# Mixture of experts over tokens sorted by expert: items of two weight chunks and 256 tokens, in place of every expert over every token

## What is computed

```python
h = x @ down_w + down_b                          # 512 -> 256
logits = x @ router_w + router_b - COST_LAMBDA * cost
probs = jax.nn.softmax(logits, axis=-1)
topv, topi = jax.lax.top_k(probs, TOP_K)         # TOP_K = 2
gate = jax.nn.softmax(topv, axis=-1)
for k in range(TOP_K):
    mask = jax.nn.one_hot(topi[..., k], E, dtype=h.dtype)
    acc = jnp.zeros_like(h)
    for e, (w1, b1, w2, b2) in enumerate(expert_params):
        hm = h * mask[..., e:e + 1]
        acc = acc + (_gelu(_gelu(hm) @ w1 + b1) @ w2 + b2)
    out = out + acc * gate[..., k:k + 1]
out = out + 0.1 * (_gelu(_gelu(h) @ shared_w1 + shared_b1) @ shared_w2 + shared_b2)
out = out @ up_w + up_b
out = out + (_gelu(x) @ core_w + core_b)
```

## Time and profile before

| | us |
|---|---|
| median of 3 runs (3240.45 to 3253.45) | 3247.59 |
| the profiled execution | 3248.38 |
| its span, first to last instruction | 3246.5 |
| the block of the mixture in it | 622.1 to 1317.6 |
| its loop over pairs | 791.4 to 1267.0 |
| PE busy over the whole span | 2938.1 (91%) |

### The profile page before, as it was taken

How to read it: one execution, slowest core, us unless ns; L and a number is a source line. 1 busy time by engine, 2 the same in 40 slices (tenths; PEclk the granted TensorE clock), 3 DMA queues, 4 the chain that set the end, 5 groups by cost and what they waited for, 6 DMA issues and landing times. The chain is left out here.

```text
span 3246.5 us, 44385 instructions
## 1 busy us (share of the span) xinstructions
PE 2938.1 (91%) x13909; PEld 1804.4 (56%) x13932; DVE 2050.6 (63%) x4083; ACT 1539.4 (47%) x3166; POOL 279.6 (9%) x248
## 2 busy tenths in 40 slices
PE   8999978799999999699899899898799999993887
PEld 4455444335999997465566655654555454432333
DVE  5666554343566665675765756755577777856776
ACT  5445332222555554254344344443477676754454
POOL 0000012002000000110210200201110101000010
PEclk9999999898999999899999999999999999995999
DMA  3000004100000000300000000000100000004000
GB/s 123 14 13 0 13 30 134 46 29 5 12 13 10 13 11 2 149 1 1 14 1 14 1 1 14 1 1 5 48 8 5 5 5 2 2 2 156 7 19 26
DMA packets 42490, 77.63 MB, mean 24 GB/s; under 512 B 6256, under 2 KB 21376, under 8 KB 39392
## 3 DMA queue, kind: packets, MB, share of 16 engines
q1 hardware_dynamic: 39440, 67.40, 5.9%
q0 software_dynamic: 2896, 8.31, 0.8%
HBM read 55.25 MB, written 4.19 MB: 18 GB/s over the span
## 5 line engine op out<-in xcount | busy, mean ns | idle before, releaser
L1890 DVE TENSOR_REDUCE x_neg_max<-bank 128x1 f32<-128x512 f32 x512 | 327.4, 684 | 95.4 <-PE bank L1735 94.8
L1842 ACT ACTIVATE x_weights<-bank 128x512 f32<-128x512 f32 x512 | 279.1, 599 | 126.9 <-PE bank L1746 122.1
L1190 PE MATMUL bank<-a_wo,a_att_cols 128*128 128x512 f32 x512 | 226.9, 594 | 6.8 <-DVE a_att_cols L1303 3.7
L1240 ACT ACTIVATE a_probs<-bank,a_neg_max 128x128 f32<-128x128 f32 (+3 forms) x256 | 138.6, 541 | 190.6 <-DVE a_neg_max L1338 190.3
L955 DVE TENSOR_TENSOR moe_hid_low<-moe_hid,moe_hid_high 128x512 fp32r<-128x512 f32 x168 | 116.4, 693 | 177.0 <-ACT moe_hid_high L825 169.7
L116 PEld LDWEIGHTS bank<-all_ident,a_probs 128*128 128x128 f32 x1216 | 155.3, 142 | 105.8 <-issue 52.5
L116 PE MATMUL bank<-all_ident,a_probs 128*128 128x128 f32 x1216 | 197.0, 275 | 17.8 <-DMA a_probs<-all_x_tok 17.8
L1232 ACT COPY a_probs_t<-bank 128x128 f32<-128x128 f32 (+3 forms) x256 | 108.8, 425 | 194.3 <-PE bank L116 194.3
L753 PE MATMUL bank<-moe_w_high,moe_hid_low 128*128 128x256 f32 x672 | 190.2, 283 | 0.0
L753 PE MATMUL bank<-moe_w_low,moe_hid_high 128*128 128x256 f32 x672 | 190.1, 283 | 0.0
L753 PE MATMUL bank<-moe_w_high,moe_hid_high 128*128 128x256 f32 x672 | 189.3, 282 | 0.1
(11 more groups left out here) (352 smaller groups left out, 6598.4 us busy)
## 6 DMA issues: line engine op xcount, KB each, us to landing
moe_w<-in_L_ffn_e_w SPq DMA_DIRECT2D x40, 128.0 KB, 2.2
all_x_tok<-in_x SPq DMA_DIRECT2D x1, 4096.0 KB, 18.2
x_x_rows<-all_x_tok SPq DMA_DIRECT2D x4, 1024.0 KB, 7.8
moe_x_rows<-all_x_tok SPq DMA_DIRECT2D x4, 1024.0 KB, 4.7
a_probs<-all_x_tok SPq DMA_DIRECT2D x4, 1024.0 KB, 4.6
a_wqkv<-in_L_attn_Wqkv SPq DMA_DIRECT2D x1, 4096.0 KB, 20.0
a_wo<-in_L_attn_Wo SPq DMA_DIRECT2D x1, 4096.0 KB, 29.6
tw_raw<-in_L_ffn_w_gate SPq DMA_DIRECT2D x4, 1024.0 KB, 7.9
```

The source lines that it names most:

```text
L1190: last = pe.matmul(mm[g % 2], att_cols[:, h % HALF_HEADS, j * P:(j + 1) * P], wo[:, h, :], start=h == first, stop=h == end - 1)
L1240: act.activation(probs[:, n % SLOTS, 0:t], sc[n % 4][:, 0:t], ACT.Exp, bias=neg_max[:, n:n + 1], accum_out=row_sum[:, n:n + 1]).then_inc(s ...
L1842: act.activation(weights[:, chunk % 2, k, :], weight_banks[slot % 2], ACT.Exp).then_inc(s.weight.free, 1)
L1890: dve.tensor_reduce(neg_max[:, g % 2, j, h:h + 1], score_banks[slot % 3], AX.X, ALU.max, negate=True) \
```

## The change

The mixture no longer runs every expert over every token. The tokens are sorted by expert, and each expert runs only over the tiles of 256 tokens that its own tokens fill.

- **Packing.** While `self_attention_0` runs, POOL issues 60 transfers from DRAM to DRAM that lay each pair of chunks (first weights, second weights, bias) together in `moe_items`, 20 pairs of 513 KB. In `cross_attention_0` POOL also loads `shared_w1` and writes zeros over `moe_sorted`, 24 tiles of 256 rows of 1 KB.
- **Routing.** The rows are turned straight from `m.x_tok`, without a load. DVE does the choice once for all 16 tiles of 128 tokens, then counts the tokens of each expert, gives every token and choice its row in the sorted order (`index`), and writes a table `which` that says, for each of the items, which tile and which pair of chunks it takes.
- **Scatter.** POOL sends each row of `gelu(h)` to its two places in `moe_sorted`, in 32 indirect transfers of 128 rows each. The shared expert is computed densely, before the items.
- **Items.** There are always 79 of them, the most that any choice of experts can need (`most_items`); an item that is not needed works on a spare tile. For each item SP reads the number of the pair from `which` into a register (`value_load`) and loads the weights in two transfers, 256 and 257 KB, into one of three slots; ACT reads the tile's number and copies the turned tile to `x_now`; PE multiplies; ACT applies the gelu; PE multiplies; DVE reads the tile's number and adds into the tile's `acc`. The tiles of sorted rows are loaded by SP, up to seven tiles ahead of the item that is being issued, and turned on PE four ahead. The products are plain 32-bit matmuls, without parts.
- **Return.** SP stores each finished tile to `moe_mixed`. When all 23 are stored, POOL gathers the rows back, in 32 indirect transfers with 8 buffers; DVE adds them, times their gates; then the sums are turned, multiplied by `up`, added and normalised tile by tile, with two layer norm buffers in turn.

What is left of the first part keeps its matmuls, in another order. The core of the diff:

```diff
-            with pool.Fori(0, B) as b:
+            layernorm_rstd(pool, st, 0, m, s)
+            pack_experts(pool, packed, a)
+            with pool.Fori(1, B) as b:
...
+            pool.memset(zeros[:], 0.0).then_inc(zeros_made, 1)
+            pool.wait_ge(zeros_made, 1)
+            pool.dma_start(packed.sorted.rearrange("(t p) d -> p t d", p=P), zeros[:].unsqueeze(1).to_broadcast([P, SUB * TILES, LATENT])) \
+                .then_inc(packed.cleared, 16)
             with pool.Fori(0, B) as b:
                 layernorm_rstd(pool, st, b, m, s)
+            pool.wait_ge(packed.cleared, 16)
...
+TOKENS = 256
...
+SPARE = (TOP_K * B * S + EXPERTS * (TOKENS - 1)) // TOKENS
+TILES = SPARE + 1
...
+def pack_experts(pool, packed, a):
+
+    for e in range(EXPERTS):
+        for n in range(PAIRS[e]):
+            to, at = packed.items[PAIR0[e] + n], slice(n * 2 * P, (n + 1) * 2 * P)
+            half = KL * LATENT
+            pool.dma_start(to[:, 0:half].rearrange("p (k n) -> p k n", k=KL), chunked(a[f"L0_ffn_e{e}_w1"][:, at])) \
+                .then_inc(packed.items_in, 16)
+            pool.dma_start(to[:, half:2 * half].rearrange("p (c n) -> p c n", c=2), chunked(a[f"L0_ffn_e{e}_w2"][at, :])) \
+                .then_inc(packed.items_in, 16)
+            pool.dma_start(to[:, 2 * half:PACKED], columns(a[f"L0_ffn_e{e}_b1"][at]), allow_slow_non_contiguous=True) \
+                .then_inc(packed.items_in, 16)
 
...
+            def load_item(i):
+                pair = sp.value_load(which[i:i + 1, 1:2], min_val=0, max_val=PAIR0[EXPERTS] - 1)
+                source = packed.items[bass.ds(pair, 1)].rearrange("o p n -> p (o n)")
+                if i >= SLOTS:
+                    sp.wait_ge(*filled(("hidden", i - SLOTS)))
+                sp.dma_start(item[:, i % SLOTS, 0:FIRST], source[:, 0:FIRST]).then_inc(s.first_in[i % SLOTS], 16)
+                if i >= SLOTS:
+                    sp.wait_ge(*filled(("item", i - SLOTS)))
+                sp.dma_start(item[:, i % SLOTS, FIRST:], source[:, FIRST:]).then_inc(s.second_in[i % SLOTS], 16)
...
+            def load_rows(n):
+                if n >= AHEAD:
+                    sp.wait_ge(*emptied(("turn", n - AHEAD)))
+                at = TURN[n] * TOKENS
+                sp.dma_start(rows_in[:, n % AHEAD, :].rearrange("p (j d) -> p j d", j=SUB),
+                             packed.sorted[at:at + TOKENS, :].rearrange("(j p) d -> p j d", p=P)).then_inc(s.rows_in[n % AHEAD], 16)
+
...
+            def store_tile(t):
+                sp.wait_ge(*emptied(("item", min((t + 1) * max(PAIRS), ITEMS) - 1)))
+
+            sp.wait_ge(packed.items_in, ITEM_LOADS)
+            sp.wait_ge(s.which_ready, 1)
+            for i in range(SLOTS):
+                load_item(i)
+            sp.wait_ge(s.scattered, TOP_K * T * 16)
+            for n in range(AHEAD + SLOTS):
+                load_rows(n)
+            stored = 0
+            for i in range(SLOTS, ITEMS):
+                if i + AHEAD < TILES:
+                    load_rows(i + AHEAD)
+                load_item(i)
+                if (stored + 1) * max(PAIRS) + SLOTS <= i:
+                    store_tile(stored)
+                    stored += 1
+            for t in range(stored, SPARE):
+                store_tile(t)
...
+            def turn_rows(n):
+                pe.wait_ge(s.rows_in[n % AHEAD], (n // AHEAD + 1) * 16)
+                pe.wait_ge(*room(("turn", n)))
                 for k in range(KL):
-                    for weight, h in ((w1_high, gh_high), (w1_high, gh_low), (w1_low, gh_high)):
-                        last = pe.matmul(hc[c], weight[:, slot, c, k, :], h[:, k, tokens], start=n == 0, stop=n == 3 * KL - 1)
-                        n += 1
+                    for j in range(SUB):
+                        last = pe.transpose(bank(("turn", n))[:, k * TOKENS + j * P:k * TOKENS + (j + 1) * P],
+                                            rows_in[:, n % AHEAD, j * LATENT + k * P:j * LATENT + (k + 1) * P], m.ident[:])
+                last.then_inc(full(("turn", n)), 1)
...
+            def hidden(i):
+                weight = item[:, i % SLOTS, 0:KL * LATENT].rearrange("p (k n) -> p k n", k=KL)
+                pe.wait_ge(s.first_in[i % SLOTS], (i // SLOTS + 1) * 16)
+                pe.wait_ge(s.x_now_ready, i + 1)
+                pe.wait_ge(*room(("hidden", i)))
+                for c in range(2):
+                    for k in range(KL):
+                        last = pe.matmul(bank(("hidden", i))[:, c * TOKENS:(c + 1) * TOKENS], weight[:, k, c * P:(c + 1) * P],
+                                         x_now[:, i % 2, k * TOKENS:(k + 1) * TOKENS], start=k == 0, stop=k == KL - 1)
+                last.then_inc(full(("hidden", i)), 1)
...
+            def output(i):
+                weight = item[:, i % SLOTS, KL * LATENT:2 * KL * LATENT].rearrange("p (c n) -> p c n", c=2)
+                pe.wait_ge(s.second_in[i % SLOTS], (i // SLOTS + 1) * 16)
+                pe.wait_ge(*emptied(("hidden", i)))
+                pe.wait_ge(*room(("item", i)))
+                for j in range(SUB):
...
-                                for n, (h, weight) in enumerate(((hid_high, w2_high), (hid_high, w2_low), (hid_low, w2_high))):
-
-                                    last = pe.matmul(to, h[:, c, tokens], weight[:, slot, c, :], start=c == j == n == 0,
-                                                     stop=c == 1 and n == 2, skip_group_check=True)
+                        last = pe.matmul(bank(("item", i))[:, j * LATENT:(j + 1) * LATENT],
+                                         hid[:, i % 2, c * TOKENS + j * P:c * TOKENS + (j + 1) * P], weight[:, c, :],
+                                         start=c == 0, stop=c == 1)
+                last.then_inc(full(("item", i)), 1)
...
+            for n in range(AHEAD):
+                turn_rows(n)
+            hidden(0)
+            for i in range(ITEMS):
+                if i + AHEAD < TILES:
+                    turn_rows(i + AHEAD)
+                if i + 1 < ITEMS:
+                    hidden(i + 1)
+                output(i)
+
+            for t in range(T):
+                pe.wait_ge(s.returned_used, (t + 1) * TOP_K)
+                pe.wait_ge(*room(("sums", t)))
+                turn_tile(pe, bank(("sums", t)), base[:, t, :], m.ident[:], KL).then_inc(full(("sums", t)), 1)
+                pe.wait_ge(*emptied(("sums", t)))
+                pe.wait_ge(*room(("up", t)))
+                for k in range(KL):
+                    last = pe.matmul(bank(("up", t)), acc_cols[:, t % 2, k * P:(k + 1) * P], w.up[:, k, :], start=k == 0, stop=k == KL - 1)
+                last.then_inc(full(("up", t)), 1)
...
+            def take_tile(i):
+                if i == 0:
+                    act.wait_ge(*filled(("base", B - 1, HALVES - 1)))
+                if i >= 2:
+                    act.wait_ge(*filled(("hidden", i - 2)))
+                act.wait_ge(*emptied(("turn", min(i + 1, TILES - 1))))
+                tile = act.value_load(which[i:i + 1, 0:1], min_val=0, max_val=SPARE)
+                act.copy(x_now[:, i % 2, :], turned[:, bass.ds(tile, 1), :].rearrange("p o n -> p (o n)")).then_inc(s.x_now_ready, 1)
...
+            for i in range(ITEMS):
+                act.wait_ge(s.second_in[i % SLOTS], (i // SLOTS + 1) * 16)
+                act.wait_ge(*filled(("hidden", i)))
+                if i >= 2:
+                    act.wait_ge(*filled(("item", i - 2)))
+                for c in range(2):
+                    last = act.activation(hid[:, i % 2, c * TOKENS:(c + 1) * TOKENS], bank(("hidden", i))[:, c * TOKENS:(c + 1) * TOKENS],
+                                          ACT.Gelu, bias=item[:, i % SLOTS, PACKED - KL + c:PACKED - KL + c + 1])
+                last.then_inc(free(("hidden", i)), 1)
+                if i + 2 < ITEMS:
+                    take_tile(i + 2)
...
+            for i in range(ITEMS):
+                if i + AHEAD < TILES:
+                    keep_turned(i + AHEAD)
+                tile = dve.value_load(which[i:i + 1, 0:1], min_val=0, max_val=SPARE)
+                to = acc[:, bass.ds(tile, 1), :].rearrange("p o n -> p (o n)")
+                dve.wait_ge(s.acc_clear, min(i + 2, TILES))
+                dve.wait_ge(*filled(("item", i)))
                 dve.drain()
+                dve.tensor_tensor(to, bank(("item", i)), to, ALU.add).then_inc(free(("item", i)), 1)
...
+            def combine(t):
+                for n, g in enumerate((g1, g2)):
+                    at = t * TOP_K + n
+                    dve.wait_ge(s.returned_in[at % RETURNED], (at // RETURNED + 1) * 16)
+                    dve.drain()
+                    dve.scalar_tensor_tensor(base[:, t, :], returned[:, at % RETURNED, :], g[:, t:t + 1], base[:, t, :], ALU.mult, ALU.add) \
+                       .then_inc(s.returned_used, 1)
...
+            pool.wait_ge(packed.cleared, 16)
+            pool.wait_ge(s.index_ready, 1)
```

(19 more changed lines are left out.)

748 lines of the change are left out of this document (442 added, 306 removed).

## The result

The changed kernel takes 3105.88 us (median of 4 runs, 3097.40 to 3111.33), against 3249.68 before (4 runs): ratio 0.9568, 95% interval 0.9551 to 0.9585, 4.3% faster. The profiled execution took 3105.17 us, its span is 3103.4. The forecast was 3120.

A forecast was written before the change was run, and what follows sets the result against it. PE's matmuls were taken to bound the old loop. Items -189.6, start to first item +35, end +22 and ahead of the block +5 sum to -128 us: 3248.4 to 3120.8, less 0.8 for the median, 3120 us; range 3095 to 3150.

The forecast's parts named there:

- no cost ahead, no wait and half of the 18 us: Lower range end: no cost ahead of the block, no wait for DVE's choice, half the end's fixed 18 us; 3095 us.
- middle rivals: Indirect transfers of about 3 us (3179 us) and items paced by something beside PE (3175 us), chance 0.15 each.
- Term 1: Item loop: 79 items of 8 matmuls at 0.436 us, PE ending last, 286 us against 475.6; -189.6 us.
- Term 2: Block start to first item: routing, shared expert and core products take 204 us against 169.3, scatter hidden; +35 us.
- Term 3: After the last item: gather, 16 tiles at 3.4 us on DVE, last norm, 72.4 us against 50.6; +22 us.
- Term 4: Ahead of the block: packing free on POOL, zeros in cross_attention_0 colliding with row fetches; +5 us.
- Indirect transfers at 3 us or more: Scatter and gather: about 3 us per transfer, 3179 us, chance 0.15; over 4.1 us, slower than before, chance 0.07.
- Items paced by something else: Item loop: register loads on ACT or SP's list set 4.2 us an item, +55 us, 3175 us; chance 0.15.
- Weight transfers that don't overlap: Item loop: two weight transfers in turn, 5.6 us per item, +156 us, 3276 us; chance 0.03.

The follow-up runs named there:

- registers_4x: Changed kernel with four register loads per item on ACT and DVE in place of one; ratio 0.9580 to the kernel before, items 283.7 us.
- items_50: Changed kernel with 50 items in place of 79; ratio 0.9292 to the kernel before, items 183.6 us.
- one_transfer: Changed kernel with each item's weights loaded in one transfer in place of two; ratio 0.9640 to the kernel before, items 309.8 us.
- scatter_twice: Changed kernel with each of the 32 scatters repeated into a second, unread DRAM tensor; ratio 0.9582 to the kernel before.

## Why the prediction was right

The time lies 14 us under the forecast, within its own range (3095 to 3150), and each step can be set beside its part of the profile. All four terms came out lower than forecast. (The prediction's own working of that range doesn't hold: no cost ahead, no wait and half of the 18 us make 3100 and not 3095, and 3150 takes in neither of the middle rivals, 3175 and 3179.)

| step | predicted | measured |
|---|---|---|
| 1, items | -189.6 | 283.8 - 475.6 = -191.8 |
| 2, start to first item | +35 | 200.6 - 169.4 = +31.2 |
| 3, end | +22 | 70.7 - 50.8 = +19.9 |
| 4, ahead of the block | +5 | -0.8 |
| sum in the span | -128 | -143.1, with -1.6 in the later stages |

**Term 1.** 8 x 0.436 us from the earlier trace rows was the whole of it. That nothing else paces the items was shown by registers_4x; that each costs 3.49 whatever it works on, by items_50 (3.46). The guess for the register load was twice too high, 0.43 to 0.5 us measured, and didn't matter, as the prediction said. A gelu of 256 took 0.47 us where "at most 0.43" stood, without effect too. And "four times an fp32r one" is too much by the prediction's own rows: 512 columns at 2.17 per ns are 0.236 us against 0.87, so 3.7 times, and an item pays 1.23 per column and not 4/3; no term was made from it.

**Term 2.** The pieces came out as 19.6 for the first sequence (22), 72.1 for three more (73), 11.3 (11.3), a wait of 3.5 (5.5), 55.0 up to the last core product (52.4), 34.7 (36) and 4.4 (4). The one that was too low has `core` 2 and 3 in it: behind PE's wait for the choice they took 9.47 us for 6.9, at the lower clock. The scatter hides, at one transfer every 1.27 us where the bound was 2.5.

**Term 3 was right by luck, as two errors met.** From the last item to DVE's first gathered row 9.1 us (10); 48.1 for the 16 tiles' products (54.4: while the first gathers come in, no share of norms and only later tiles' adds are due); from the last product to the last norm 10.0 (8). Then 3.5 us that no part of the term had: POOL's drain. 6.3 us too many for the tiles stand against 5.5 too few behind them. At the end of this block it took 0.98 us before, so the stretch that the term was made from didn't have it. But POOL issued no transfer there, and in the stage ahead, where it issues the loads of the earlier trace rows, the line of the block's end showed one in the kernel before:

```profile
L391 POOLq DRAIN  x1: 3487/3487/3487, 618.3 to 618.3; - x1
```

The change brings transfers of POOL into the last stretch of a block; the rows of the one block that already had them should have been read for its end.

**Term 4 missed a cost, and its measured size is chance.** The packing's issues are free, as forecast: POOL's second layer norm stands at 243.8, 0.3 us behind the earlier trace rows, and they took 0.69 us each. But the packing isn't free. The line of the end of `self_attention_0`, before and after:

```profile
L162 POOLq DRAIN  x1: 989/989/989, 473.5 to 473.5; - x1
```

```profile
L163 POOLq DRAIN  x1: 5903/5903/5903, 472.1 to 472.1; - x1
```

POOL's drain takes 5.90 us there and not 0.99 (4.9 behind POOL's last work, again 0.08 for each of the 60 transfers), 300 us after the last of them was issued, and the next block begins 3.1 us behind DVE's last norm and not 0.1. All the runs with the packing have this drain, 5.90 to 5.91 us. These 3 us are the same cost as in term 3, at a second place, and the prediction had it at neither.

In `cross_attention_0` the zeros landed in 22.8 us; the transfers of rows in that stage took 9.1 us and not 7.8 (medians of four), and PE's last product there didn't move. POOL's drain fell from 3.49 to 0.91 us, so that DVE ends the stage: the next block begins 0.2 us behind DVE and not 1.1. This is the one place where the drain doesn't follow the count (37 transfers). POOL waits for its zeros as its last act there, but it also stands idle for 12.94 us ahead of issuing them, and which of the two makes the drain short isn't shown: in the mixture POOL waits for its scatters too, and more of these made the drain longer. The 5 us were put on a collision without asking whether the rows' transfer had slack.

The -0.8 in the table is one profile against one: in the 13 profiles with the new kernel's first two stages the block of the mixture begins anywhere from 618.9 to 624.8, before at 622.0.

**The rivals.** Indirect transfers at 3 us or more: out by the lines of L1283 and L1299. Items paced by something else: out by registers_4x, and for SP by PE's 0.4 us of idle time. Weight transfers that don't overlap: the earlier trace rows had 2.2 us for the old ones, they now land in 3.0 to 3.2 us, and PE waits for none. The Trainium skill, "DMA: Bandwidth & Descriptors", section "Anatomy of one DMA — SWDGE (gpsimd) path", has 2.0 us plus bytes over 436 GB/s for a transfer issued by GpSimd, 2.6 us for 256 KB as an estimate; those here are issued by SP and land in 3.0 to 3.2. That they run one after another was the prediction's addition and isn't on the page, and the trace disagrees with it: PE is idle for 0.4 us over 158 of them. one_transfer shows that larger pieces are worse here, because of when they may be asked for.

What the prediction didn't see is how near the cover of the rows was: rows asked for three tiles later cost 118 us, twice the price of either middle rival.

## What to carry to other kernels

Where one engine is busy all through a loop, the price of a changed loop is its instructions times the price of one from the timeline, and spare items count in full; a list whose length is fixed for the worst case costs the difference, here 100 us of 284. Look, for each transfer that moves with the loop, at how long before its use it may be asked for; a wait of 4 us in each of 19 turns cost half as much again as it lasted, because PE came out of it at its lower clock. Where POOL issues transfers, look at the end of that block, even where they landed long before: its drain can end last. And before work is put into an engine's wait, ask whose bank or buffer it needs, and who frees that.

## What the runs showed of the hardware

- POOL's drain at a block's end lasts longer the more transfers POOL has issued in the block, even where the last was issued 300 us before: beyond POOL's last work 0.1 us with none, 2.9 with 35 loads, 4.9 with 60 transfers from DRAM to DRAM, 5.3 with 64 indirect ones and 7.9 with 96 (scatter_twice), some 0.08 us each. The exception is `cross_attention_0` after the change, 0.2 us with 37, where POOL waits for a transfer of its own at the end. It hides if POOL's list ends early.
- A register load from SBUF takes 0.27 to 0.31 us, with its register operations 0.43 to 0.50.
- An indirect transfer of 128 rows of 1 KB costs POOL 0.96 us (scatter) or 0.95 us (gather), one every 1.25 to 1.27, and lands after 2.4 (scatter) or 2.7 us (gather).
- The same stage, with the same instructions, was granted a clock of 0.86 to 0.89 or of 0.75 in its first 61 us in different profiles, and took 663 to 664 or 670 us. In the two profiles with 0.75 a saving of 18 or 100 us upstream lost 6 of it there.
- In one kernel PE's records came 2.1 to 2.8 us apart for 18 us, and DVE was idle for up to 12.6 us between adds that were due, with no wait that the trace names; why stays open.
